# Two-layer graph network on one core: row factors made on TensorE, score subtractions between the first steps, the first pair in two tiles, and matmuls without a reader in TensorE's waits

## What is computed

```python
h = maximum(layernorm(x), 0)
A = (adj != 0)
x = x + A @ (h @ W0 + b0) / sum(A, axis=0)[:, None]
h = maximum(layernorm(x), 0)
ht = (h @ W1) per head                       # 4 heads of 512
src, dst = ht . a_src, ht . a_dst            # one number per head and row
e = leaky_relu(src[:, :, None] + dst[:, None, :], 0.01) + adj
x = x + mean over heads of softmax(e) @ ht
```

## Time and profile before

| | |
|---|---|
| median of 3 runs | 2495.39 us (2494.52 to 2496.39) |
| the profiled execution | 2494.08 us, its span 2492.3 us |
| PE busy | 2447.1 us (98%) |
| VectorE busy | 1866.4 us (75%) |
| ScalarE busy | 1258.9 us (51%) |
| granted TensorE clock, mean | 0.995 |

### The profile page before, as it was taken

How to read it: one execution, slowest core, us unless ns; L and a number is a source line. 1 busy time by engine, 2 the same in 40 slices (tenths; PEclk the granted TensorE clock), 3 DMA queues, 4 the chain that set the end, 5 groups by cost and what they waited for, 6 DMA issues and landing times.

```text
span 2492.3 us, 42728 instructions
## 1 busy us (share of the span) xinstructions
PE 2447.1 (98%) x12328; PEld 1198.3 (48%) x12328; DVE 1866.4 (75%) x2560; ACT 1258.9 (51%) x1883; POOL 49.3 (2%) x44
## 2 busy tenths in 40 slices
PE   6999999799999999999999999999999999999999
PEld 3544447344444444444444444444444444444787
DVE  7588767876688766877668776687766887667776
...
DMA packets 74223, 144.21 MB, mean 58 GB/s; under 512 B 4489, under 2 KB 11915, under 8 KB 72970
## 3 DMA queue, kind: packets, MB, share of 16 engines
...
## 4 chain that ended last, share of the span: by engine, by line
PE 94%; DVE 3%; DMA 1%; issue 1%; ACT 1%; SPq 0%; DVEq 0%; ACTq 0%
PE z_ps L731 70%; PE o_ps L759 11%; PE o_ps L1351 3%; PE z_ps L1351 3%; PE z_ps L1404 2%; PE c_ps L1322 1%; PE o_ps L1322 1%; DMA ring_reg<-adjT_in 1%; PE c_ps L1351 1%; DVE hl_reg L917 1%; PE c_ps L1383 1%; PE o_ps L1375 0%; PE o_ps L1309 0%; DMA h_reg<-x_in 0%; DVE w_reg L952 0%
## 5 line engine op out<-in xcount | busy, mean ns | idle before, releaser
L731 PE MATMUL z_ps<-hl_reg,h_reg 128*128 (+2 forms) x8736 | 1759.0, 364 | 11.1 <-DVE hl_reg L608 11.1
L731 PEld LDWEIGHTS z_ps<-hl_reg,h_reg 128*128 (+1 forms) x8736 | 855.2, 98 | 911.4 <-DVE hl_reg L608 11.4
L559 ACT ACTIVATE hl_reg<-t_reg (+2 forms) x364 | 361.9, 994 | 731.5 <-DVE t_reg L635 379.4
L608 DVE TENSOR_TENSOR hl_reg<-t_reg,hl_reg (+2 forms) x364 | 417.6, 1147 | 235.0 <-ACT hl_reg L559 233.3
L544 ACT ACTIVATE t_reg<-ring_reg,vv 128x512 f32 (+3 forms) x728 | 526.3, 770 | 66.0 <-DVE ao_reg L623 60.3
L635 DVE SCALAR_TENSOR_TENSOR t_reg<-t_reg,vv,e_reg (+3 forms) x728 | 510.3, 743 | 7.7 <-issue 7.7
L623 DVE TENSOR_TENSOR ao_reg<-ao_reg,t_reg 128x1024 f32<-128x1024 f32 (+1 forms) x336 | 383.7, 1142 | 0.0
L759 PE MATMUL o_ps<-w_reg,z_reg 128*128 128x512 f16 x1248 | 278.2, 379 | 0.9 <-DVE z_reg L651 0.9
L759 PEld LDWEIGHTS o_ps<-w_reg,z_reg 128*128 128x128 f16 x1248 | 119.8, 98 | 140.9 <-DVE z_reg L651 1.2
L651 DVE SCALAR_TENSOR_TENSOR z_reg<-z_ps,z_reg 128x512 f16<-128x512 f32 (+1 forms) x112 | 73.2, 653 | 151.6 <-ACT z_reg L571 151.6
L456 ACT ACTIVATE e_reg<-e_reg (+2 forms) x91 | 90.1, 996 | 152.0 <-DVE e_reg L467 151.9
...
## 6 DMA issues: line engine op xcount, KB each, us to landing
...
```

Of the source, the lines that this page charges most:

```text
L559: nc.scalar.activation(hl_ring[:, g % HL_RING, 0, :, 0:W], t_ring[:, g % T_RING, :, 0:W], ACT.Copy).then_inc(hi_ready, 1)
L608: nc.vector.tensor_tensor(hl_ring[:, g % HL_RING, 1, :, 0:W], t_ring[:, g % T_RING, :, 0:W], hl_ring[:, g % HL_RING, 0, :, 0:W], ALU.subtr ...
L731: mm = nc.tensor.matmul(z_ps[:, k, 0:W], hk[hs], hl_ring[:, r, ps, u, 0:W], start=first and u == 0 and n == 0, stop=last and u == 1 and n ...
```

## The change

1. The scores are no longer scaled and copied: maximum and sums read them in `c_ps`, and the factor 1/`HS` goes into the scale of ScalarE's exponentials.
2. The exponentials go to `ev`; two operations write all three forms of `vv`, with `PS`. The mask of valid rows comes later, in the first step.
3. The row factors of head 0 of block 0 no longer go through DRAM: TensorE transposes each column of `rows_c`, spread over 128 columns (4 transposes), into `o_ps[:, 1]`, and ScalarE copies it into `c_bc[:, 0]`. The way through DRAM stays for the other heads; ScalarE's copy for it (`c_rows`) comes after step 1 of layer 1.
4. The first pair goes tile by tile: ScalarE, VectorE and TensorE each work on its tile 0, then on its tile 1.
5. Exponentials and subtractions of pairs 3 to 6 are put between the first steps, and the split of pairs 11 and 12 behind step 4.
6. TensorE gets matmuls whose result nobody reads (`keep_clock`, 512 columns each, into `o_ps[:, 2]`): 14 before the last transpose, 12 after the last scores, 14 before layer 1's first matmul.

```diff
-        sdc = ao_reg[:, NP:NP + NT * 2 * H]
+        ev = ao_reg[:, NP:NP + NT * 2 * H]
-        c_st = t_reg[:, 0:P]
+        c_st = max_st
...
         def layer2_scalar(act, c_rows, high1):
                 if isinstance(p, int) and p == 0:
-                    act.wait_ge(c_in[h], (b + 1) * 16)
+                    if isinstance(b, int) and b == 0 and h == 0:
+                        act.wait_ge(c0_sb, 1)
+                        act.wait_ge(s_vvp, 2)
+                    else:
+                        act.wait_ge(c_in[h], (b + (h > 0)) * 16)
...
                 for p in range(2, LOOP0):
                     step(b, h, p)
+                    if isinstance(b, int) and b == 0 and h == 0:
+                        exp_e(act, 0, E_PRE0 + p - 1)
+                if isinstance(b, int) and b == 0 and h == 0:
+                    for j in range(LATE_SPLIT, PAIRS):
+                        high1(j)
...
             t1(0, 0, 0)
-            for p in range(2):
-                step(0, 0, p)
+            for u in range(2):
+                act.wait_ge(p_ready, u + 1)
+                nc.scalar.activation(hl_ring[:, 0, 0, u], t_ring[:, 0, u],
+                                     ACT.Copy).then_inc(f_hi if u == 0 else hi_ready, 1)
+            t1(0, 0, 1)
+            step(0, 0, 1)
+            exp_e(act, 0, E_PRE0)
+            c_rows()
...
                 for p in range(4, LOOP0):
                     step(b, h, p)
+                    if isinstance(b, int) and b == 0 and h == 0:
+                        subtract_max(dve, 0, E_PRE - 1)
+                        for j in range(LATE_SPLIT, PAIRS):
+                            split1(j)
...
-            for p in range(4):
-                step(0, 0, p)
+            step(0, 0, 0)
+            for u in range(2):
+                if u == 0:
+                    dve.wait_ge(f_hi, 1)
+                else:
+                    dve.wait_ge(hi_ready, 1)
+                nc.vector.tensor_tensor(hl_ring[:, 0, 1, u], t_ring[:, 0, u], hl_ring[:, 0, 0, u],
+                                        ALU.subtract).then_inc(f_lo if u == 0 else lo_ready, 1)
+            last = vv[:].rearrange("p (r t) -> p r t", t=NT)[:, :, NT - 1]
+            nc.vector.tensor_scalar(last, last, valid[:, NT - 1:NT], None, ALU.mult).then_inc(s_vmask, 1)
+            accumulate(0, 0, 0)
+            for p in range(1, 4):
+                step(0, 0, p, before=(0, 0, p - 1) if p > 1 else None, lone=p == 1)
+                subtract_max(dve, 0, E_PRE0 + p - 1)
...
-            pair(0, 0, 0, first=True)
+            for u in range(2):
+                if u == 0:
+                    pe.wait_ge(f_lo, 1)
+                else:
+                    pe.wait_ge(lo_ready, 1)
+                for k in range(KT):
+                    for n, (hs, ps) in enumerate(((0, 0), (0, 1), (1, 0))):
+                        mm = nc.tensor.matmul(z_ps[:, k], h16[:, u, hs, k * P:(k + 1) * P], hl_ring[:, 0, ps, u],
+                                              start=u == 0 and n == 0, stop=False)
+            mm.then_inc(hl_free, 1)
...
-                link(dve, nc.vector.tensor_scalar(sdc, c_ps[:, 0:NT * 2 * H], 1.0 / HS, None, ALU.mult))
...
-                for h in range(H):
+                for h in range(1, H):
                     load_c(sp, 0, h)
...
+                def keep_clock(n):
+
+                    for i in range(n):
+                        nc.tensor.matmul(o_ps[:, 2], h16[:, 0, 0, 0:P], h16[:, 0, 0], start=True, stop=True)
```

More of the change, by code:

```diff
@@ L199, in gnn_kernel @@
         c_ps = ctx.enter_context(nc.psum_tensor("c_ps", [P, 512], F32))
+        sd_rt = c_ps[:, 0:NT * 2 * H].rearrange("p (t r) -> p r t", r=2 * H)
+        sd4 = c_ps[:, 0:NT * 2 * H].rearrange("p (t h r) -> p h r t", h=H, r=2)
         s_var = sem("s_var")
@@ L349, in gnn_kernel @@
         s_vv = sem("s_vv")
+        s_vvp = sem("s_vvp")
+        s_vmask = sem("s_vmask")
+        cb_ps = sem("cb_ps")
+        c0_sb = sem("c0_sb")
+        f_hi = sem("f_hi")
+        f_lo = sem("f_lo")
         s_carg = sem("s_carg")
@@ L534, in layer2_gpsimd, with layer2_scalar @@
             blocks(pool, body)
-        def layer2_scalar(act):
+        def layer2_scalar(act, c_rows, high1):
             def t1(b, h, p):
@@ L623, in accumulate, with step @@
                     nc.vector.tensor_tensor(acc, acc, tp, ALU.add).then_inc(acc_done, 1)
-            def step(b, h, p, before=None):
+            def step(b, h, p, before=None, lone=False):
                 W = width(b)
                 g = (b * H + h) * PAIRS + p
-                before = before or ((b, h, p - 1) if not isinstance(p, int) or p > 0 else None)
+                if not lone:
+                    before = before or ((b, h, p - 1) if not isinstance(p, int) or p > 0 else None)
                 if h == 0:
@@ L1133, in _ @@
                 dve.wait_ge(sd_ps, NT)
[L1134 to L1136 removed]
+                nc.vector.tensor_reduce(dmx[:], sd_rt, AX_X, ALU.max).then_inc(s_dmx, 1)
                 dve.wait_ge(s_dall, 1)
                 dh = dall[:].rearrange("p (h r) -> p h r", r=2)[:, :, 1:2].broadcast_to((P, H, NT))
[L1139 to L1140 removed]
+                nc.vector.tensor_tensor(dn3, sd4[:, :, 1], dh, ALU.subtract).then_inc(s_dn, 1)
+                link(dve, nc.vector.tensor_tensor(qq3, sd4[:, :, 0], dh, ALU.add))
                 link(dve, nc.vector.scalar_tensor_tensor(out=lk3, in0=qq3, scalar=SLOPE, in1=qq3,
@@ L1145, in _ @@
                 dve.wait_ge(s_vv, 2)
-                link(dve, nc.vector.tensor_scalar(vv[:].rearrange("p (r t) -> p r t", t=NT)[:, 0:2 * H, NT - 1],
-                                                  vv[:].rearrange("p (r t) -> p r t", t=NT)[:, 0:2 * H, NT - 1],
-                                                  valid[:, NT - 1:NT], None, ALU.mult))
-                link(dve, nc.vector.tensor_scalar(vv[:, 0:2 * H * NT], vv[:, 0:2 * H * NT], PS, None, ALU.mult))
-                link(dve, nc.vector.tensor_scalar(vv4[:, 2], vv4[:, 0], -1.0, None, ALU.mult))
-                for p in range(E_PRE0, E_PRE):
-                    subtract_max(dve, 0, p)
-                for j in range(LATE_SPLIT, PAIRS):
-                    split1(j)
-                layer2_vector(dve)
+                nc.vector.tensor_scalar(vv4[:, 2], ev4[:, 0], -PS, None, ALU.mult).then_inc(s_vvp, 1)
+                nc.vector.tensor_scalar(vv[:, 0:2 * H * NT], ev, PS, None, ALU.mult).then_inc(s_vvp, 1)
+                dve.wait_ge(s_vvp, 2)
+                layer2_vector(dve, split1)
             @block.scalar
@@ L1286, in _ @@
                 transposed1(NT - 1)
-                for p in range(E_PRE0):
+                for p in range(E_PRE0 - 1):
                     exp_e(act, 0, p)
@@ L1290, in _, with c_rows @@
                 for q, f in ((0, 1.0), (1, SLOPE)):
-                    nc.scalar.activation(vv4[:, q], dn3, ACT.Exp, scale=f).then_inc(s_vv, 1)
+                    nc.scalar.activation(ev4[:, q], dn3, ACT.Exp, scale=f / HS).then_inc(s_vv, 1)
                 act.wait_ge(s_carg, 1)
-                nc.scalar.activation(cc3, cc3, ACT.Exp).then_inc(s_cexp, 1)
-                act.wait_ge(cr_ps, 1)
-                nc.scalar.activation(c_st[0:H * NT], o_ps[0:H * NT, 0, 0:P], ACT.Copy).then_inc(cr_sb, 1)
-                for j in range(LATE_SPLIT, PAIRS):
-                    high1(j)
-                for p in range(E_PRE0, E_PRE):
-                    exp_e(act, 0, p)
-                layer2_scalar(act)
+                nc.scalar.activation(cc3, cc3, ACT.Exp, scale=1.0 / HS).then_inc(s_cexp, 1)
+                exp_e(act, 0, E_PRE0 - 1)
+                act.wait_ge(cb_ps, 1)
+                act.wait_ge(x1_out[0], 16 * sum((NA + i) % ADJ_RING == 0 for i in range(PAIRS)))
+                nc.scalar.activation(c_bc[:, 0], o_ps[:, 1], ACT.Copy).then_inc(c0_sb, 1)
+                def c_rows():
+                    act.wait_ge(mr_out, 16)
+                    act.wait_ge(cr_ps, 1)
+                    nc.scalar.activation(c_st[0:H * NT], o_ps[0:H * NT, 0, 0:P], ACT.Copy).then_inc(cr_sb, 1)
+                layer2_scalar(act, c_rows, high1)
             @block.tensor
@@ L1428, in _ @@
                                 scores(i - 1)
+                def keep_clock(n):
+                    for i in range(n):
+                        nc.tensor.matmul(o_ps[:, 2], h16[:, 0, 0, 0:P], h16[:, 0, 0], start=True, stop=True)
                 scores(NT - 2)
+                pe.wait_ge(mr_sb, 1)
+                pe.wait_ge(st1_split, 1)
+                keep_clock(14)
                 transpose1(NT - 1)
                 scores(NT - 1)
+                keep_clock(12)
                 pe.wait_ge(s_cexp, 1)
                 pe.wait_ge(tr_sb, NT)
+                for t in range(IT):
+                    mm = nc.tensor.transpose(o_ps[:, 1, t * P:(t + 1) * P], rows_c[:, t:t + 1].broadcast_to((P, P)),
+                                             ident[:])
+                mm.then_inc(cb_ps, 1)
```

(1 more changed line is left out.)

9 lines of the change are left out of this document (2 added, 7 removed).

## The result

The changed kernel took 2491.58 us in the median of 20 runs (2488.66 to 2495.96), the kernel before 2495.34 (20 runs). The ratio is 0.9983, 95% interval 0.9977 to 0.9989: 0.17% faster, 3.8 us in the medians, where 3.9 was forecast. The profiled execution took 2490.59 us.

A forecast was written before the change was run, and what follows sets the result against it. PE bounds the kernel, busy 98% of the span. Of 8.6 + 2.1 us gained, 4.6 are given back, leaving 6.0; minus 2.1 for the clock gives 3.9 us less, 2491.4 against the median, range 2488.0 to 2494.2.

The forecast's parts named there:

- Start: Between the layers: layer 1's first matmul 8.6 us earlier, at 449.82, and at the full clock, worth another 2.1 us.
- DRAM or queue: Ahead of layer 1's first step: ScalarE's queue, not mainly the way through DRAM, was the hold; start 446.80, not 453.22.
- Given back: VectorE's list up to lo of pair 4, 27.45 us: TensorE waits 1.3 us at pair 1, 3.3 at pair 4; 4.6 lost.
- The cycle of the loop: Layer 1 behind pair 4: VectorE's cycle takes 4.91 us against PE's 5.18, so no further wait.
- The clock in the new wait: Wait at pair 4: clock lost, costing 2.1 us, chance 0.5; rival, clock survives, 6.0 us less in all, chance 0.27.
- The clock between the layers: Rival, chance 0.13: around layer 0's last tile the clock falls despite the fillers; 2.2 us remain as gain, 2493.2.
- The sum: Whole kernel: pair 4 starts 6.0 us earlier, minus 2.1 for the lost clock, gives 3.9 us less, 0.16%.

The follow-up runs named there:

- moving the work: The change with the subtraction of pair 3 and splits and roundings of pairs 11 and 12 moved into idle time: 2487.72 us, ratio 0.9961 to the kernel before.
- The second profile: The changed kernel measured again without any edit: median 2493.51 us of 11 runs, ratio 0.9988 to the kernel before.

## Why the prediction was right, step by step

- **Start.** t1 at x1 + 10.9 forecast, 10.8 measured; first matmul 13.9 and 13.9. Two errors within cancelled, and that is luck. Reads of PSUM were not slower: from the maximum to the last sum it took 1.95 us (444.94 to 446.89), 0.6 less than I had by adding 0.33 to a sum in which the same operations on SBUF took 2.25. But the exponential of the factors didn't start then: ScalarE came out of its two exponentials only at 447.01, at the date that I had computed for it, and did the two of the column factors ahead (0.45 us), which the sum didn't have. I had called it "in time".
- **DRAM or queue.** "What is bypassed there is not mainly the way through DRAM" was wrong: each held t1 alone nearly as long (16.6 and 17.5, before 17.3). The number was unaffected, since the change removes both.
- **Given back.** Waits at pair 1 of 1.3 forecast and 1.32 measured, at pair 4 of 3.3 and 3.10; pair 4 at x1 + 39.2 and 39.4. VectorE's list from its first p to the end of lo of pair 4 was summed at 27.45 us and took 27.4 (450.06 to 477.43), of which the wait for `high1` was 2.07 and not 2.16. The cause is shown by moving the work: of 4.4 us of waits 0.3 were left, and PE's list puts none of it down to VectorE.
- **The cycle of the loop.** 4.91 us forecast where nothing holds it up; after the wait VectorE's subtractions follow at 477.35, 482.26 and 487.17, 4.91 apart, until TensorE holds them again.
- **The clock in the new wait.** Chance 0.5 against 0.27: one of two profiles lost it, at 3.0 us where 2.1 was forecast. The half-speed stretch was 5.9 us, longer than the 4.21 before from which I took the price.
- **The clock between the layers.** This rival, at 0.13, was probably rated too low: of ten profiles with fillers behind the scores, six had the clock fall within them, though neither of the two of the change itself. Its price was rated too high, 1.2 us in t1 and not 3.85, because the clock came back while the fillers ran: 12 took 4.44 us and not 5.1.
- **The sum.** 3.9 us forecast, 3.8 measured. By the two profiles the median is one of a mixture of handovers 5.8 and 2.9 us shorter than before, with layer 0's own scatter on top, so the agreement to 0.1 us is luck. So is that of the profiled execution (2490.2 forecast, 2490.59): it kept the clock, and its layer 0 ended 2.4 us later. The first term of the sum, 6.0 us, measured 5.8 and is no luck; the second, 2.1 us for the lost clock, measured 3.0.

The traces agree with the Trainium skill, page "VectorE: DVE Perf Modes", section "Why PSUM operands drop a tier", that PSUM holds fp32 operands to the single rate: the sums and the maximum, which have the single rate anyway, lost nothing by reading PSUM (L1185 0.27 us, and 0.34 for the same sum from SBUF before). By that rule the 0.11 us that I took for the price of PSUM in the earlier trace rows would be the scaling's loss of its double rate; no run here tests this alone. The Trainium skill, page "TensorE: Matmul & The Clock Gate", section "HAM oscillation — how this bites in real kernels", says that a long gap is paid again each time. The second profile agrees, the first, on the same dates, does not.
